# First attention: slot weights and values in tiles of 32 columns, scores and slot scores in tiles of 64

## The chip, the cores and the metric

The kernel runs on one core of a Trainium2 chip. The metric is the device time of one execution in microseconds; the median of some executions stands for a kernel. Within the core, TensorE (PE in the profile) multiplies matrices. Its weight loads (PEld) are instructions of their own and overlap the matmuls. VectorE (DVE), ScalarE (ACT) and GpSimd (POOL) work beside it; they wait for each other by semaphores.

## The reference, cut to what matters

The program is two transformer layers on `x` of 64 sequences, 32 tokens each, 256 channels. The change lies in the first attention, with 16 heads of 128 channels and 64 slots per head. Tokens see only their own sequence, and there only themselves and earlier tokens:

```python
A = jnp.einsum('bhtd,bhjd->bhtj', q, k) * scale      # scores
A = jnp.where(mask, A, 0.0)
ok = enz * jnp.einsum('bhtj,bhjm->bhtm', A, es)      # slot scores
qv = jax.nn.softmax(ok, axis=-1)
W2 = jnp.einsum('bhtm,bhjm->bhtj', qv * enz, es)     # slot weights
W2 = jnp.where(mask, W2, 0.0)
o = jnp.einsum('bhtj,bhjd->bhtd', W2, v)             # values
```

`mask` is lower triangular over the 32 tokens (T = 32) of a sequence. `A` and `W2` are therefore 32 x 32 matrices, one for each sequence and head.

## The kernel before

`attention0` works in 64 steps. A step `i` takes 128 token rows (one of G = 16 groups, four whole sequences, BPG = 4) and four of the heads (HQ = 4). The steps run over the 16 groups within each of the four quads of heads. Every engine has its own list of instructions, written out by hand and executed in order; what crosses engines is a semaphore wait.

In a step TensorE does, in this order (function, line): the transposes of the softmax (`turn_p`, L372), half of the output projection (`heads_out`, L420), the transposes of the gated output (`turn_og`, L372), **the slot weights** (`slot_weights`, L437), the other half of the output projection (L420), the transposes of `es` (`turn_es`, L372), **the scores** of the next step (`scores`, L391), **the values** (`values`, L449), **the slot scores** of the next step (`slot_scores`, L403), then one matmul for the slots (L362), the projections of v and gate (`project`, L330, twelve matmuls), and those of q and k (`quarter`, L319, twelve) with the running sums (L367, L368) in their middle.

The four functions in bold multiply many small matrices, and each places them in a part of the 128 x 128 array with `tile_position` (first row, first column of the array). All four use tiles of 64 x 64, which hold two sequences at once. The product of two sequences' tokens is 64 x 64, of which only the two diagonal blocks of 32 x 32 are wanted; the masks `mA` and `m01_own` (128 x 64 each) put zeros on the rest. `scores` and `slot_weights` take their 64 contracted rows from either half of the partitions (`e`) and write tokens to either half of the columns (`b`), four tiles in all; `slot_scores` and `values` contract over the 64 tokens of a pair of sequences, so only the two tiles on the diagonal are used.

A matmul of type f32 stands in the trace as two matmul and two weight-load records; one of type fp32r as one of each (the trace prints both as f32 on some lines). So 8 slot-weight matmuls are 16 records of L437.

VectorE multiplies the scores in PSUM by `mA` into `am` (`mask_scores`, L714), and the slot weights by `m01_own` into `wm` (`mask_weights`, L719). The scores and the slot weights share a pair of PSUM banks (`pair`, AW_TA in the trace), so `scores` waits for `mask_weights` (`w2_mask`). ScalarE copies v out of PSUM (`v_out`, L507, v_s) before TensorE may start `quarter` on the same bank.

Of the kernel before, what the change touches and what calls it, by code (L numbers as in the profile page):

```python
# [10 lines left out]
ALU = mybir.AluOpType  # L11
# [3 lines left out]
P = 128  # L15
B, T, D = 64, 32, 256
BPG = P // T
# [4 lines left out]
H0, DK, M0 = 16, 128, 64  # L22
HQ = 4
# [15 lines left out]
def attention0(nc, k, xres, x, cond, wcond, w_slices, wo, ws1, ws2b, ucol, gnorm, rope_cos, rope_sin, maskA, mask01, mask01_own):  # L39

    with ExitStack() as ctx:
        sb, psum, sem = k.tools(ctx)
# [4 lines left out]
        TW2 = 2 * T  # L47
# [19 lines left out]
        sinb = sb("sinb", [P, T])  # L67
        mA = sb("mA", [P, TW2])
        m01 = sb("m01", [P, P])
        m01_own = sb("m01_own", [P, TW2])  # L70
        idx_i = sb("idx_i", [B, 1], I32)
        u_col = sb("u_col", [RW, 1])
        turned = sb("turned", [P, 2, 2, 2, 2, TOK])
# [11 lines left out]
        enz = sb("enz", [P, SW])  # L85
        esT_s = sb("esT_s", [P, SW])
        am = sb("am", [P, HQ, TW2])
        wm = sb("wm", [P, HQ, TW2])
        ok = sb("ok", [P, SW])
        ex = sb("ex", [P, SW])  # L90
        exz = sb("exz", [P, SW])
# [3 lines left out]
        pT_s = sb("pT_s", [P, SW])  # L95
# [9 lines left out]
        pair = psum("AW_TA", [P, 2, QW])  # L105
# [12 lines left out]
        def heads(ap, n=HQ):  # L118
            return ap.rearrange("p (h d) -> p h d", h=n)

        both = pair[:, :, 0:2 * TW2].rearrange("p e (a t) -> p a e t", a=2)

        def by_pairs(ap):
            return ap[:, :, :].rearrange("p (a e) t -> p a e t", a=2)

        def for_heads(mask):
            return mask[:, :].unsqueeze(1).unsqueeze(1).to_broadcast([P, 2, 2, TW2])

        def turn_of(j):

# [36 lines left out]
        a_mm, a_mask = sem("a_mm"), sem("a_mask")  # L167
        ok_mm, ok_z, ok_min, ok_exp = [sem(n) for n in ("ok_mm", "ok_z", "ok_min", "ok_exp")]
        p_sum, p_eps, p_z = sem("p_sum"), sem("p_eps"), sem("p_z")
        w2_mm, w2_mask = sem("w2_mm"), sem("w2_mask")  # L170
# [119 lines left out]
        def _(pe):  # L290
# [3 lines left out]
            for g in range(G):  # L294
                if g == G // 2:
                    pe.wait_ge(x_more, 16)
                for c in range(KD):
                    m = pe.matmul(banks[g // 2][:, (g % 2 * KD + c) * P:(g % 2 * KD + c + 1) * P],
                                  xres[:, g, c * P:(c + 1) * P], bd[:, g, :], start=True, stop=True)
# [129 lines left out]
            def slot_weights(i):  # L429
                pe.wait_ge(pT_ev, i + 1)  # L430
                pe.wait_ge(esT_ev, i + 1)
                for a in range(2):
                    for b in range(P // TW2):
                        own = slice(a * P + b * TW2, a * P + (b + 1) * TW2)
                        for e in range(2):
                            rows = slice(e * M0, (e + 1) * M0)
                            m = pe.matmul(pair[b * TW2:(b + 1) * TW2, e, a * TW2:(a + 1) * TW2], esT_s[rows, own], pT_s[rows, own],  # L437
                                          start=True, stop=True, tile_position=(e * M0, b * TW2))
                m.then_inc(w2_mm, 1)

            def values(i):
                pe.wait_ge(w2_mask, i + 1)
                pe.wait_ge(v_ev, i + 1)
                pe.wait_ge(o_gate, i)
                pe.wait_ge(o_sq, i)
                for h in range(HQ):
                    for b in range(P // TW2):
                        toks = slice(b * TW2, (b + 1) * TW2)
                        m = pe.matmul(OO[toks, h * P:(h + 1) * P], wm[toks, h, :], v_s[toks, i % 2, h * P:(h + 1) * P],  # L449
                                      start=True, stop=True, tile_position=(b * TW2, b * TW2))  # L450
                m.then_inc(o_mm, 1)

            A = slice(0, None)
# [17 lines left out]
            for i in range(-1, STEPS):  # L471
                now, one, two = i >= 0, i + 1 < STEPS, i + 2 < STEPS
                if now:
                    turn_p(i)
                if i >= 2:
                    heads_out(i - 2, (0, 2))
                if i >= 1:
                    turn_og(i - 1)
                if now:
                    slot_weights(i)  # L480
                if i >= 2:
                    heads_out(i - 2, (2, HQ))
                if one:
                    turn_es(i + 1)
                    scores(i + 1)
                if now:
                    values(i)
                if one:
                    slot_scores(i + 1)
                if two:  # L490
                    slots(i + 2)
                if one:
                    proj_v(i + 1, A)
                    proj_g(i + 1, A)
                x1(i + 1 + FIRST)
                if two:
                    running(i + 2)
                x2(i + 1 + FIRST)
# [114 lines left out]
        def _(dve):  # L613
# [97 lines left out]
            def mask_scores(i):  # L711
                dve.wait_ge(a_mm, i + 1)
                dve.wait_ge(ok_mm, i)
                dve.tensor_tensor(by_pairs(am), both, for_heads(mA), ALU.mult).then_inc(a_mask, 1)  # L714

            def mask_weights(i):
                dve.wait_ge(w2_mm, i + 1)
                dve.wait_ge(o_mm, i)
                dve.tensor_tensor(by_pairs(wm), both, for_heads(m01_own), ALU.mult).then_inc(w2_mask, 1)  # L719

            for j in range(FIRST):
                x1_by_cos(j)
# [8 lines left out]
            for i in range(-1, STEPS):  # L731
                j, now, one, two = i + 1 + FIRST, i >= 0, i + 1 < STEPS, i + 2 < STEPS
                if now:
                    mask_weights(i)
                if now and one:
                    z(i + 1, 1)
                if i >= 2:
                    y_out(i - 2)
                if one:
                    mask_scores(i + 1)  # L740
                    slot_max(i + 1)
                if two:
                    clip(i + 2)
                if now:
                    norm_sum(i)
                    gated(i)
                if one:
                    slot_sum(i + 1)
                    silu(i + 1)
                if j < TURNS:  # L750
                    x1_by_cos(j)
                    x1_by_sin(j)
                if two:
                    z(i + 2, 0)
                if j < TURNS:
                    x2_by_both(j)
# [1224 lines left out]
def build(nc, a, out):  # L1981
    with ExitStack() as whole:
# [28 lines left out]
        with nc.Block() as block:  # L2011
            @block.sync
            def _(sp):
# [3 lines left out]
                sp.wait_ge(first, 48)  # L2017

        attention0(nc, k, xres, *[a[n] for n in ATT0])
        renew()  # L2020
        raw = sb("raw", [P, 3, KD * 1024])
# [61 lines left out]
def constants():  # L2083

    import numpy as np

    def rotary(width):
        inv = 1.0 / np.float32(10000.0) ** (np.arange(0, width, 2, dtype=np.float32) / width)
        angle = np.arange(T, dtype=np.float32)[:, None] * inv[None].astype(np.float32)
        c, s = np.cos(angle), np.sin(angle)  # L2090
        return np.tile(np.concatenate([c, c], 1), (BPG, 1)), np.tile(np.concatenate([-s, s], 1), (BPG, 1))

    j, t = np.arange(P)[:, None], np.arange(P)[None]
    seen = ((j // T == t // T) & (j <= t)).astype(np.float32)
    own = np.tile(seen[0:2 * T, 0:2 * T], (P // (2 * T), 1))
    inv0 = 1.0 / np.float32(10000.0) ** (np.arange(0, DK, 2, dtype=np.float32) / DK)
    turn0 = np.tile((np.arange(T, dtype=np.float32)[:, None] * inv0[None].astype(np.float32)).T, (2, 1))
    cos1, sin1 = rotary(4)
    later = np.where(np.arange(T)[None] > np.arange(T)[:, None], np.float32(-1e30), np.float32(0))
    return {  # L2100
        "identity": np.eye(P, dtype=np.float32), "ucol": (np.arange(RW) % (2 * RQ) == RS).astype(np.float32).reshape(RW, 1),
        "slot": np.where(np.arange(3 * 16) // 16 == 1, -1, np.arange(3 * 16) % 16).astype(np.float32).reshape(3 * 16, 1),
        "pcol": (np.arange(P) // 16).astype(np.float32).reshape(P, 1), "prow": np.arange(P, dtype=np.float32).reshape(P, 1),
        "rope_cos": np.cos(turn0), "rope_sin": np.sin(turn0),
        "mask_scale": own * np.float32(DK ** -0.5), "mask01": seen, "mask01_own": own,
        "cneg": np.tile(later, (BPG, 1)), "rcos1": cos1, "rsin1": sin1,
    }

# [16 lines left out]
```

## Time and profile before

| | us |
|---|---|
| median of 3 runs | 1463.17 |
| lowest, highest | 1461.98, 1464.67 |
| the profiled execution: its time | 1463.88 |
| its span in the profile | 1462.1 |
| PE busy | 1332.1 (91%) |
| PEld busy | 1065.6 (73%) |
| DVE busy | 938.1 (64%) |
| ACT busy | 517.3 (35%) |
| POOL busy | 556.4 (38%) |

The profile's times start at the beginning of the span; 1.8 us of the execution lie around it. The steps of the first attention fill the stretch from about 63 to 783 us. What follows (the first MLP, the second attention, the second MLP) is not touched by the change, and serves below only as a place where other sizes of tile can be seen. In a timeline row the first number is the start, the second the time from the first start to the last end of a merged group; matmul records overlap, so the pace is read from one group's start to the next group's start.

### The profile page before, as it was taken

The page shows a single profiled execution, that of the slowest core. Times are in us where ns is not written, and L with a number is a line of the kernel's source. Part 1 is how long each engine was busy: PE and PEld are TensorE (multiplying, and loading weights), DVE is VectorE, ACT ScalarE, POOL GpSimd, SP SyncE. Part 2 cuts the span into 40 slices and gives each one's busy share as a digit, 9 for nine tenths or more (in the row PEclk, how much of TensorE's full clock was granted, in tenths as well). Part 3 has the DMA queues.
Part 4 walks back from the last instruction along what each step waited for, and adds up shares of the span by engine and source line. Part 5 has one row for each costly group of instructions (what it writes and reads, how often), then busy time and mean ns, then how long its engine had stood idle before and what let it go on. Part 6 is the DMA issues. An engine that isn't in the chain of part 4 may idle for free. (4 is left out here: it accounts for less than half of the span.)

```text
span 1462.1 us, 36841 instructions
## 1 busy us (share of the span) xinstructions
PE 1332.1 (91%) x14806; PEld 1065.6 (73%) x14806; DVE 938.1 (64%) x1825; ACT 517.3 (35%) x1188; POOL 556.4 (38%) x608
## 2 busy tenths in 40 slices
PE   2899999999999999999986789999998788997996
PEld 2688888888888888888864577777776566775664
DVE  2787887888788878787864464252424245666786
ACT  2244444444444444444442213231312122222442
POOL 0665555565656565555531312122221111122111
PEclk9999999999999999999998899999999799997998
DMA  6000000000000000000002500000000630000610
GB/s 192 5 12 13 13 13 13 30 13 12 13 16 27 13 13 17 1 2 2 1 2 95 163 1 1 0 1 0 0 0 0 206 90 0 0 0 15 198 58 22
DMA packets 33376, 46.47 MB, mean 32 GB/s; under 512 B 6974, under 2 KB 22552, under 8 KB 32728
## 3 DMA queue, kind: packets, MB, share of 16 engines
q1 hardware_dynamic: 31048, 42.23, 9.5%
q10 hardware_dynamic: 2112, 2.10, 0.5%
q8 instruction: 93, 1.52, 0.4%
q14 instruction: 43, 0.35, 0.1%
q0 software_dynamic: 80, 0.26, 0.1%
HBM read 42.22 MB, written 2.36 MB: 30 GB/s over the span
## 5 line engine op out<-in xcount | busy, mean ns | idle before, releaser
L420 PE MATMUL OE<-w_o,ogT_s 128*128 128x256 f32 x512 | 139.5, 396 | 0.7 <-ACT ogT_s L507 0.7
L876 POOL TENSOR_TENSOR hT_lo<-h,hT_hi 128x512 fp32r<-128x512 f32 x44 | 56.8, 1291 | 192.9 <-ACT hT_hi L1049 192.9
L234 POOL TENSOR_TENSOR turned<-t1c,t2s 128x512 f32<-128x512 f32 x62 | 78.7, 1269 | 122.2 <-DVE t2s L637 122.2
L662 DVE RECIPROCAL enz<-SC 128x128 f32<-128x128 f32 x128 | 121.2, 948 | 2.9 <-PE SC L368 2.5
L1112 DVE SCALAR_TENSOR_TENSOR t<-th,m 128x512 f32<-128x512 f32 (+1 forms) x56 | 38.4, 685 | 121.3 <-ACT th L1054 93.5
L275 POOL TENSOR_TENSOR exz<-ex,enz 128x256 f32<-128x256 f32 x64 | 47.4, 741 | 160.9 <-ACT ex L573 160.9
L319 PE MATMUL PJ<-hs_hi,w_hi 128*128 128x512 f32 x248 | 102.4, 413 | 0.0
L330 PE MATMUL PJ<-w_hi,hs_hi 128*128 128x512 f32 x256 | 100.5, 392 | 0.0
L330 PE MATMUL PJ<-w_hi,hs_lo 128*128 128x512 f32 x256 | 100.1, 391 | 0.0
L330 PE MATMUL PJ<-w_lo,hs_hi 128*128 128x512 f32 x256 | 99.9, 390 | 0.0
L420 PEld LDWEIGHTS OE<-w_o,ogT_s 128*128 128x128 f32 x512 | 88.2, 192 | 12.4 <-ACT ogT_s L507 1.0
L319 PE MATMUL PJ<-hs_hi,w_lo 128*128 128x512 f32 x248 | 97.1, 392 | 0.0
L319 PE MATMUL PJ<-hs_lo,w_hi 128*128 128x512 f32 x248 | 96.9, 391 | 0.0
L573 ACT ACTIVATE ex<-ok,mn 128x64 f32<-128x64 f32 x256 | 68.3, 337 | 52.6 <-DVE mn L701 52.6
L507 ACT ACTIVATE pT_s<-AW_TA 128x256 f32<-128x256 f32 x64 | 24.6, 384 | 167.0 <-PE AW_TA L372 167.0
L1049 ACT ACTIVATE hT_hi<-h 128x512 fp32r<-128x512 f32 (+1 forms) x56 | 35.4, 632 | 124.4 <-DVE h L1118 124.4
L235 POOL TENSOR_TENSOR turned<-t2c,t1s 128x512 f32<-128x512 f32 x62 | 78.6, 1268 | 0.0
L242 POOL TENSOR_TENSOR og<-og,rstd 128x512 f32<-128x512 f32 x64 | 66.6, 1041 | 5.0
L449 PE MATMUL OO<-v_s,wm 64*64 64x128 f32 x1024 | 67.7, 269 | 0.0
L1308 POOL TENSOR_TENSOR r<-qk,raw 128x128 f32<-128x128 f32 x16 | 7.4, 463 | 156.5 <-DVE qk L1537 156.5
L239 POOL TENSOR_TENSOR rstd<-mse,mhalf 128x4 f32<-128x4 f32 x64 | 65.1, 1017 | 4.9 <-DVE mse L691 4.9
L666 DVE SCALAR_TENSOR_TENSOR gs<-gs,PJ 128x512 f32<-128x512 f32 x64 | 44.0, 687 | 34.6 <-ACT gs L528 34.6
(383 smaller groups left out, 3575.1 us busy)
## 6 DMA issues: line engine op xcount, KB each, us to landing
we_ring<-in_we SPq DMA_DIRECT2D x64, 256.0 KB, 3.1
w_raw<-in_w_slices SPq DMA_DIRECT2D x48, 128.0 KB, 2.2
turned<-in_w_slices ACTq DMA_DIRECT2D x4, 512.0 KB, 7.4
xres<-in_x SPq DMA_DIRECT2D x2, 1024.0 KB, 14.6
out_rows<-xres SPq DMA_DIRECT2D x16, 128.0 KB, 1.7
w1r<-in_w1i SPq DMA_DIRECT2D x1, 1408.0 KB, 6.5
w_s<-in_w SPq DMA_DIRECT2D x2, 682.0 KB
w_o<-in_wo SPq DMA_DIRECT2D x1, 1024.0 KB, 5.3
```

Source lines behind the costliest of these rows:

```text
L234: pool.tensor_tensor(to[:, 0, :], x1c[:, :], x2s[:, :], ALU.subtract)
L235: pool.tensor_tensor(to[:, 1, :], x2c[:, :], x1s[:, :], ALU.add).then_inc(qk_add, 1)
L239: pool.tensor_tensor(rstd[:, :], mse[:, :], mhalf[:, :], ALU.pow).then_inc(o_rstd, 1)
L242: pool.tensor_tensor(heads(og[:, :]), heads(og[:, :]), rstd[:, :].unsqueeze(2).to_broadcast([P, HQ, DK]), ALU.mult).then_inc(o_norm, 1)
L275: pool.tensor_tensor(exz[:, :], ex[:, :], enz[:, :], ALU.mult).then_inc(p_z, 1)
L319: m = pe.matmul(banks_of(j)[half][:, :], w[:, slot, a:a + P], h[:, c, toks], start=(n == 0), stop=(n == len(terms) - 1))
L330: m = pe.matmul(bank[:, :], h[:, c, toks], w[:, slot, a:a + QW], start=(n == 0), stop=(n == len(terms) - 1))
L420: m = pe.matmul(OE[:, SW:SW + D], ogT_s[:, i % 2, h * P:(h + 1) * P], w_o[:, i // G % 2, h, :], start=(h == 0), stop=(h == HQ - 1))
L449: m = pe.matmul(OO[toks, h * P:(h + 1) * P], wm[toks, h, :], v_s[toks, i % 2, h * P:(h + 1) * P], start=True, stop=True, tile_position=(b ...
L573: act.activation(ex[:, cols], ok[:, cols], ACT.Exp, scale=-1.0, bias=mn[:, h:h + 1]).then_inc(ok_exp, 1)
L662: dve.reciprocal(enz[:, cols], SC[:, SW:2 * SW][:, cols]).then_inc(z_rec, 1)
L876: eng.tensor_tensor(hT[1][s, m % 2, :], h[s, m % 2, :], hT[0][s, m % 2, :].bitcast(F32), ALU.subtract).then_inc(second, 1)
```

## The change

`slot_weights` and `values` go to tiles of 32 columns, one sequence each. The slot weights become 16 matmuls of 64 rows x 32 columns with 32 columns streamed (before 8 of 64 x 64 with 64), in eight tiles. The values become 16 matmuls of 32 x 32 with 128 columns streamed (before 8 of 64 x 64 with 128), in the four tiles on the diagonal. `wm` and the mask `m01_own` shrink from 64 to 32 columns, so `mask_weights` works on 128 x 128 instead of 128 x 256 elements; the view `both` takes its width as an argument. `scores`, `slot_scores` and `mA` stay as they are. The file is longer by one line, so numbers of lines from 122 on are one higher afterwards.

```diff
-        m01_own = sb("m01_own", [P, TW2])
+        m01_own = sb("m01_own", [P, T])
...
-        wm = sb("wm", [P, HQ, TW2])
+        wm = sb("wm", [P, HQ, T])
...
-        both = pair[:, :, 0:2 * TW2].rearrange("p e (a t) -> p a e t", a=2)
+        def both(width):
+            return pair[:, :, 0:2 * width].rearrange("p e (a t) -> p a e t", a=2)
...
-            return mask[:, :].unsqueeze(1).unsqueeze(1).to_broadcast([P, 2, 2, TW2])
+            return mask[:, :].unsqueeze(1).unsqueeze(1).to_broadcast([P, 2, 2, mask.shape[1]])
...
-                    for b in range(P // TW2):
-                        own = slice(a * P + b * TW2, a * P + (b + 1) * TW2)
+                    for b in range(BPG):
+                        own = slice(a * P + b * T, a * P + (b + 1) * T)
                         for e in range(2):
                             rows = slice(e * M0, (e + 1) * M0)
-                            m = pe.matmul(pair[b * TW2:(b + 1) * TW2, e, a * TW2:(a + 1) * TW2], esT_s[rows, own], pT_s[rows, own],
-                                          start=True, stop=True, tile_position=(e * M0, b * TW2))
+                            m = pe.matmul(pair[b * T:(b + 1) * T, e, a * T:(a + 1) * T], esT_s[rows, own], pT_s[rows, own],
+                                          start=True, stop=True, tile_position=(e * M0, b * T))
...
-                    for b in range(P // TW2):
-                        toks = slice(b * TW2, (b + 1) * TW2)
+                    for b in range(BPG):
+                        toks = slice(b * T, (b + 1) * T)
                         m = pe.matmul(OO[toks, h * P:(h + 1) * P], wm[toks, h, :], v_s[toks, i % 2, h * P:(h + 1) * P],
-                                      start=True, stop=True, tile_position=(b * TW2, b * TW2))
+                                      start=True, stop=True, tile_position=(b * T, b * T))
...
-                dve.tensor_tensor(by_pairs(am), both, for_heads(mA), ALU.mult).then_inc(a_mask, 1)
+                dve.tensor_tensor(by_pairs(am), both(TW2), for_heads(mA), ALU.mult).then_inc(a_mask, 1)
...
-                dve.tensor_tensor(by_pairs(wm), both, for_heads(m01_own), ALU.mult).then_inc(w2_mask, 1)
+                dve.tensor_tensor(by_pairs(wm), both(T), for_heads(m01_own), ALU.mult).then_inc(w2_mask, 1)
...
-        "mask_scale": own * np.float32(DK ** -0.5), "mask01": seen, "mask01_own": own,
+        "mask_scale": own * np.float32(DK ** -0.5), "mask01": seen, "mask01_own": own[:, 0:T] + own[:, T:2 * T],
```

On TensorE, from the transposes of the softmax to the matmul for the slots, in a step in the middle of the first attention. Each row gives the line, the output and its operands, the size of the output and how many matmuls stand in a row. Before:

```order
L372 MATMUL AW_TA<-ident,exz 128x128 x2
L420 MATMUL OE<-w_o,ogT_s 128x256 x2
L372 MATMUL TB<-ident,og 128x128 x4
L437 MATMUL AW_TA<-pT_s,esT_s 64x64 x8
L420 MATMUL OE<-w_o,ogT_s 128x256 x2
L372 MATMUL TB<-ident,es 128x128 x2
L391 MATMUL AW_TA<-turned 64x64 x16
L449 MATMUL OO<-v_s,wm 64x128 x8
L403 MATMUL OE<-es,am 64x64 x8
L362 MATMUL SC<-w_s,uT 128x256
```

On TensorE, the same place after the change:

```order
L373 MATMUL AW_TA<-ident,exz 128x128 x2
L421 MATMUL OE<-w_o,ogT_s 128x256 x2
L373 MATMUL TB<-ident,og 128x128 x4
L438 MATMUL AW_TA<-pT_s,esT_s 32x32 x16
L421 MATMUL OE<-w_o,ogT_s 128x256 x2
L373 MATMUL TB<-ident,es 128x128 x2
L392 MATMUL AW_TA<-turned 64x64 x16
L450 MATMUL OO<-v_s,wm 32x128 x16
L404 MATMUL OE<-es,am 64x64 x8
L363 MATMUL SC<-w_s,uT 128x256
```

Nothing moves; two groups have twice as many matmuls. The slot weights still stand between groups that use the whole array, but the values, in tiles of 32, now stand between two groups in tiles of 64.

## Rows read from the trace of the kernel before

**Rows 1.** Busy time of each engine in two stretches, with the granted clock (PEclk)
```profile
core 0: us, PE busy (x) PEld busy (x) DVE busy (x) ACT busy (x) POOL busy (x), PEclk, DMA share, GB/s
400.00:411.27 11.27, 11.27 (x134) 9.31 (x127) 9.03 (x18) 4.99 (x14) 7.77 (x9) 1.00 0.05 13
83.00:782.00 699.00, 689.94 (x7587) 568.02 (x7587) 549.33 (x1100) 304.60 (x789) 397.07 (x414) 1.00 0.04 12
```
**Rows 2.** Waits of TensorE's weight loads, 83 to 782 us: total us, times, longest
```profile
PEld PJ L319 <- ACT v_s L507: 13.9, 57, 0.3
PEld AW_TA L391 <- issue: 10.8, 62, 0.5
PEld AW_TA L437 <- issue: 10.4, 62, 0.2
```
**Rows 3.** Timeline of TensorE's matmuls in one step: start us, length us
```profile
407.42 0.38 PE L372 MATMUL AW_TA<-ident,exz 128*128 128x128 f32 x2
407.63 1.03 PE L420 MATMUL OE<-w_o,ogT_s 128*128 128x256 f32 x4
408.50 0.60 PE L372 MATMUL TB<-ident,og 128*128 128x128 f32 x4
409.03 0.46 PE L437 MATMUL AW_TA<-pT_s,esT_s 64*64 64x64 f32 x16
409.42 1.13 PE L420 MATMUL OE<-w_o,ogT_s 128*128 128x256 f32 x4
410.39 0.38 PE L372 MATMUL TB<-ident,es 128*128 128x128 f32 x2
410.70 0.69 PE L391 MATMUL AW_TA<-turned 64*64 64x64 f32 x32
...
412.09 0.62 PE L403 MATMUL OE<-es,am 64*64 64x64 f32 x15
```
**Rows 4.** The same, one step earlier, from the slot scores on
```profile
400.81 0.64 PE L403 MATMUL OE<-es,am 64*64 64x64 f32 x16
401.39 0.39 PE L362 MATMUL SC<-w_s,uT 96*128 96x256 f32 x1
401.61 0.39 PE L330 MATMUL PJ<-w_hi,hs_hi 128*128 128x512 f32 x1
```
**Rows 5.** Timeline of the weight loads of that step
```profile
409.02 0.33 PEld L437 LDWEIGHTS AW_TA<-pT_s,esT_s 64*64 64x64 f32 x16 [0.17 <-issue]
...
410.70 0.56 PEld L391 LDWEIGHTS AW_TA<-turned 64*64 64x64 f32 x32 [0.17 <-issue]
411.16 0.87 PEld L449 LDWEIGHTS OO<-v_s,wm 64*64 64x64 f32 x16
411.98 0.61 PEld L403 LDWEIGHTS OE<-es,am 64*64 64x64 f32 x16
```
**Rows 6.** Timeline of VectorE in that step, the two masks
```profile
409.56 0.42 DVE L719 TENSOR_TENSOR wm<-AW_TA,m_own 128x256 f32<-128x256 f32 x1 [0.25 <-PE AW_TA L437]
...
411.46 0.42 DVE L714 TENSOR_TENSOR am<-AW_TA,mA 128x256 f32<-128x256 f32 x1 [0.34 <-PE AW_TA L391]
```
**Rows 7.** Timeline of TensorE in the first step, the scores
```profile
73.37 0.69 PE L391 MATMUL AW_TA<-turned 64*64 64x64 f32 x32 [0.53 <-DVE wm L719]
73.86 1.08 PE L449 MATMUL OO<-v_s,wm 64*64 64x128 f32 x16
74.73 0.67 PE L403 MATMUL OE<-es,am 64*64 64x64 f32 x16
```
**Rows 8.** Timeline of TensorE in the second MLP: tiles of 64 rows, then 32 columns
```profile
1405.94 0.38 PE L1762 MATMUL Y<-be_s,hot_t 48*128 48x256 f32 x1
1406.26 1.07 PE L1766 MATMUL Y<-we_ring,xT 128*32 128x256 f32 x16
1407.26 0.44 PE L1752 MATMUL XY<-ident,xres 128*128 128x128 f32 x2
```
**Rows 9.** Timeline of TensorE in the second attention, tiles of 32 columns
```profile
1251.99 1.29 PE L1392 MATMUL S<-kT,qT 16*32 16x32 f32 x128
1253.64 0.59 PE L1360 MATMUL A<-xT,raw 128*128 128x128 f32 x3 [0.36 <-issue]
```
**Rows 10.** Timeline of TensorE in the first MLP, 42 rows after 128 rows
```profile
1057.76 0.40 PE L910 MATMUL m<-uum_hi,bu_lo 128*128 128x512 f32 x1
1057.99 0.39 PE L910 MATMUL m<-uum_lo,bu_hi 128*128 128x512 f32 x1
1058.31 0.39 PE L951 MATMUL m<-tern,hT_hi 42*128 42x256 f32 x1
```

## Prediction

> **What bounds the kernel now.** I read the stretches by engine first. In a step of the first attention TensorE is busy for all of its 11.27 us, at a granted clock of 1.00 (the 2.4 GHz level), while VectorE is busy for 9.03, GpSimd for 7.77 and ScalarE for 4.99 [rows 1]. Over 83 to 782 us, 62 steps, TensorE is busy 689.94 of 699.00 us. So the step is as long as TensorE's list of instructions, and the question is what the change does to that list. The waits of TensorE come next: one on another engine repeats in every step, the weight load of `quarter` that waits for ScalarE's copy of v (13.9 us in 57 times, 0.24 each); the other two that repeat are "issue" waits of 0.17 us, in front of the scores and of the slot weights [rows 2, 5]. Those two are what this change hangs on: they wait for no engine, and they stand exactly where the list goes from the whole array to tiles of 64.
>
> **The price of going from one size of tile to another.** Take the timeline of one step [rows 3]. Into tiles: two transposes take 407.63 - 407.42 = 0.21 us, so the four that start at 408.50 should hand over at 408.93; the slot weights start at 409.03, 0.10 late. Inside the tiles the second record of each matmul comes late once as well, since its weights weren't loaded ahead. The scores show that: 32 records take 411.21 - 410.70 = 0.51 us (the values start where their loads do, 411.16 to 411.21 [rows 5]), and at the pace of the slot scores, below, the 32 would take 0.46; that is 0.05. Out of tiles: the slot scores take 401.39 - 400.81 = 0.58 us [rows 4]. Their 16 records stream half of the columns that the values' 16 do, and the values take 74.73 - 73.86 = 0.87 [rows 7], some 0.054 a record; so the slot scores' own time is 0.44 to 0.46, and the step out 0.11 to 0.14. The first matmul behind it then holds the second up: the four records of the output projection take 1.13 us right behind the slot weights and 1.03 elsewhere [rows 3], 0.10 more. An excursion into tiles thus costs 0.15 in and 0.21 out.
>
> Is the same paid between two sizes of which neither is the whole array? No row of the first attention shows it. From scores to values to slot scores, all in 64 x 64, the loads show no idle time: the values' start at 411.16, before the scores end, and the slot scores' at 411.98 [rows 5]. The second MLP has the nearest place: a matmul of 48 rows is followed by tiles of 128 x 32. The first starts at 1405.94, the next at 1406.26, 0.32 later [rows 8]. The slots' matmul has the same 256 columns in one record, also stands first behind a step out of tiles, and hands over within the whole array after 401.61 - 401.39 = 0.22 [rows 4]. So 0.10 is paid there. That the number of rows alone is enough I read in the first MLP: 1058.31 - 1057.99 = 0.32 in front of 42 rows, and 0.23 in front of another 128 rows [rows 10]. I take it that 64 x 64 to 32 x 32 pays as well.
>
> The Trainium skill, TensorEngine Tiling (Array Packing), "Key Properties", says that a change of the tiling mode, not of the tile alone, drains TensorE. By that rule the values now cost two drains which they did not before; [rows 8] agrees with its 0.10 us.
>
> **The change part by part, for one step.** *Values.* Each tile still streams four heads of 128 columns, in two records each. With four tiles in place of two the records double, and four run side by side instead of two, so the 0.87 us stay. Less is excluded, since each tile streams as long as before; the upper end is that only two of the four tiles run at once, 1.74. That four tiles can share the array is seen in [rows 8]: 16 records of 256 columns in 1407.26 - 1406.26 = 1.00 us, where one after another, at the (408.50 - 407.63)/4 = 0.22 of such a record [rows 3], they would take 3.5. I take 0.
>
> *The two switches around the values.* In: 0.11, as late as elsewhere, and nothing for the second record, whose turn comes only 0.109 (0.87/8) later anyway, more than the load takes. Out, into the slot scores: 0.10, and 0.05 for the late second record, since these stream only 64 columns. Together 0.26. Bounds: 0 if 64 to 32 costs nothing, and 0.15 + 0.21 = 0.36 if each end costs what the costliest one does. I take 0.26 because [rows 8], another pair of partial sizes, shows a first part in full.
>
> *Slot weights.* They stand between whole-array groups before and after, so no switch is added. Before, 409.42 - 409.03 = 0.39 us, of which 0.11 to 0.15 is the step out [rows 3]. After there are 32 records of half the columns. The nearest row is the second attention's: 128 records of 32 columns within 1.29 us, of which about 0.19 is the last one's length, so 1.10/128 = 8.6 ns each [rows 9]; 32 of them take 0.28, less some 0.03 because the last tiles stream half as long on the way out. 0.28 + 0.11 - 0.03 = 0.36: a gain of 0.03. Bounds: a gain of 0.13 if half the columns halve the 0.25 that lies before the step out, and a loss of 0.23 if 32 records take what the 32 of the scores take, 0.51 + 0.11 against 0.39. I take -0.03, since [rows 9] has the same number of columns.
>
> *Mask of the weights on VectorE.* 0.42 us for 128 x 256 now; half of the elements, I put it at 0.25 to 0.30. It ends at 409.98 and the scores, which wait for it, start at 410.70 [rows 3, 6], so 0.7 us cover it and the gain is nothing. Only in the first two steps, where the output projection is missing, do the scores wait for it (0.53 in the first [rows 7], and once more): -0.3 us in all. If that cover fell away TensorE would wait, not gain. The mask of the scores (0.42, from 411.46) stays; the slot scores load at 411.98, right behind it [rows 5, 6]. It is released by the scores, so with the values later it gets more slack, not less. The load of `m01_own` is once, at the start, and half as large: nothing.
>
> *The wait for v.* It does not absorb the loss: ScalarE's copy of v stands behind the exponentials, these behind VectorE's work on the slot scores, all of it later by the same amount as TensorE. If it were fixed to something earlier, up to 0.09 a step would be hidden, 6 us.
>
> **The sum.** 63 steps have values between scores and slot scores: 63 x 0.26 = +16.4. 64 slot weights: 64 x -0.03 = -1.9. First steps: -0.3. Together +14.2 us, a step of 11.27 + 0.23 = 11.50. The profiled execution would go from 1463.88 to 1478.1 and its span from 1462.1 to 1476.3; the median is 0.7 lower, 1477.4. By the bounds, 0.15 to 0.36 for the switches (0 is rival 1) and -0.13 to +0.23 for the slot weights: 0.02 to 0.59 a step, 1464 to 1500.
>
> **The rivals.** (1) *No switch between 64 and 32.* The array may keep both sizes as one mode. For it: nothing in this kernel shows that very pair; against it [rows 8, 10]. Then only the slot weights' gain stays, -1.9 - 0.3: 1461. Chance 0.12. (2) *The same, and the slot weights run at full pace,* the case on the other side: with the 0.13 of their bound TensorE is that much shorter a step, and as it bounds the step [rows 1], 64 x 0.13 + 0.3 = 8.6 us come out, 1455. It decides for "faster" from 0.04 a step. It needs the switch to be free, as (1). Chance 0.05. (3) *Only two diagonal tiles run at once.* 0.87 more a step, 64 x 0.87 + 14 = +70: 1533. For it: [rows 8] has its four tiles in one block of rows, the values have four blocks of rows. Against it: the scores already use two blocks of rows and two of columns. Chance 0.05. (4) *Every small matmul has a floor.* The slot weights' 32 records would pay it one by one; against it the 8.6 ns in [rows 9]. At 27 ns a record, half of what one of the values' takes now, they would take 0.86 + 0.11 instead of 0.39: 0.58 a step, +37; with the switches' 16, 1516. The Trainium skill, TensorEngine Tiling, "Instruction Overhead", gives about 60 cycles for each matmul however few its columns; [rows 9] is against it for tiles that run side by side. Chance 0.03.
>
> **How the numbers follow.** The forecast, slower by about 14 us, gets 0.75, the rivals 0.25 as above. About 0.2% (3 us) is what a measurement can tell from no change. Slower: 0.75 + 0.05 + 0.03 = 0.83; same: 0.12; faster: 0.05. The range: 0.68 of the forecast's 0.75 lies within 1466 to 1488 (ends where both terms are at their bounds together are unlikely), and rival (1) at 1461 brings it to 0.80; above, (3), (4) and the forecast's tail are left out, below (2). So 1461 to 1488.
>
> **What would show it.** In the new profile: a step of 11.50 us; an "issue" wait or a gap of 0.1 in front of the values' weight loads and again in front of the slot scores'; the scores' start to the values' start 0.62 instead of 0.51; values to slot scores 0.97 instead of 0.87; slot weights to output projection 0.36; the mask of the weights below 0.30 us; the wait for v unchanged at 0.24. If the values' loads still start before the scores end, rival (1) holds. If values to slot scores takes 1.7, rival (3).

## The result, and the profile after

The change makes the kernel slower, as forecast, by a little less than forecast.

| | before | after |
|---|---|---|
| median us (6 runs each) | 1463.05 | 1475.5 |
| lowest, highest | 1461.2, 1464.67 | 1475.05, 1480.13 |
| ratio after / before, 95% interval | | 1.009, 1.0075 to 1.0105 |
| the profiled execution: its time, its span | 1463.88, 1462.1 | 1480.13, 1478.3 |

The forecast median was 1477.4, the measured one is 1475.5: +12.4 us instead of +14.2. The profiled execution of the kernel after is 4.6 us above its own median. Those microseconds don't lie in the changed stage. The values' matmul records (L449 before, L450 after, since the file is a line longer) end with a last start at 777.9 us before and 790.0 after, +12.1; what is left of the span behind them is 684.2 and 688.3 us, of code that the change doesn't touch. I therefore argue from the steps, whose length repeats from one to the next, and not from the span.

The last start stands in the view of one line's instructions, here that of the kernel before and then that of the kernel after:

```profile
L449 PE MATMUL OO<-v_s,wm x1024: 269/269/320, 73.9 to 777.9; 64*64 64x128 f32 x171
```

```profile
L450 PE MATMUL OO<-v_s,wm x2048: 264/268/292, 73.5 to 790.0; 32*32 32x128 f32 x187
```

The timeline of TensorE in one step after, to be read against [rows 3, 4] (start us, length us):

```profile
403.01 0.36 PE L438 MATMUL AW_TA<-pT_s,esT_s 64*32 64x32 f32 x32
403.30 1.13 PE L421 MATMUL OE<-w_o,ogT_s 128*128 128x256 f32 x4
404.26 0.38 PE L373 MATMUL TB<-ident,es 128*128 128x128 f32 x2
404.57 0.69 PE L392 MATMUL AW_TA<-turned 64*64 64x64 f32 x32
405.20 1.07 PE L450 MATMUL OO<-v_s,wm 32*32 32x128 f32 x32
406.20 0.68 PE L404 MATMUL OE<-es,am 64*64 64x64 f32 x16
406.82 0.39 PE L363 MATMUL SC<-w_s,uT 96*128 96x256 f32 x1
...
412.86 0.38 PE L373 MATMUL AW_TA<-ident,exz 128*128 128x128 f32 x2
```

| from start to start, us | before | after | difference (median over the steps, before rounding) |
|---|---|---|---|
| slot weights to output projection | 0.39 | 0.29 | -0.11 |
| scores to values | 0.51 | 0.63 | +0.11 |
| values to slot scores | 0.87 | 1.00 | +0.13 |
| slot scores to the slots' matmul | 0.58 | 0.62 | +0.04 |
| the step (softmax transposes at 401.40 to 412.86; before, [rows 1]) | 11.27 | 11.46 | +0.19 |

A step is 0.19 longer, and 63 steps of that are 12.0 us, which is what was measured. The four differences add up to 0.17 of it. The other 0.02 lie in the projections, where some matmuls follow each other a few ns later than before; why is open.

The weight loads of the same step show the mechanism. Against [rows 5], the slot scores' loads, which used to start before the values were done, now have an "issue" wait of 0.20 us; the values' loads start only at 405.20, with the values themselves:

```profile
404.57 0.56 PEld L392 LDWEIGHTS AW_TA<-turned 64*64 64x64 f32 x32 [0.17 <-issue]
405.20 0.81 PEld L450 LDWEIGHTS OO<-v_s,wm 32*32 32x32 f32 x32
406.20 0.54 PEld L404 LDWEIGHTS OE<-es,am 64*64 64x64 f32 x16 [0.20 <-issue]
```

And the waits of the weight loads over 83 to 790 us have one row more than [rows 2], the second one here. The wait for ScalarE's copy of v is nearly as it was:

```profile
PEld PJ L320 <- ACT v_s L508: 12.6, 57, 0.3
PEld OE L404 <- issue: 12.3, 62, 0.2
PEld AW_TA L392 <- issue: 10.6, 62, 0.4
PEld AW_TA L438 <- issue: 10.4, 62, 0.2
```

VectorE's mask of the weights takes 0.29 us instead of the 0.42 in [rows 6], and is over at 403.83, long before the scores at 404.57:

```profile
403.54 0.29 DVE L720 TENSOR_TENSOR wm<-AW_TA,m_own 128x128 f32<-128x128 f32 x1 [0.26 <-PE AW_TA L438]
```

### The profile page after: what moved, and what is told of

Read it like the earlier page. It is cut to its first block and busy times, and to the rows that moved or that the text cites. A ratio compares the mean times of both kernels' runs of the same rounds, so it can differ in the third digit from the quotient of the medians.

```text
span 1478.3 us, 40937 instructions
## 1 busy us (share of the span) xinstructions
PE 1347.6 (91%) x16854; PEld 1062.0 (72%) x16854; DVE 929.8 (63%) x1825; ACT 518.9 (35%) x1188; POOL 557.4 (38%) x608
## 5 line engine op out<-in xcount | busy, mean ns | idle before, releaser
L699 DVE SCALAR_TENSOR_TENSOR ok<-OE,enz 128x256 f32<-128x256 f32 x64 | 27.2, 425 | 75.4 <-PE OE L404 75.4
L450 PE MATMUL OO<-v_s,wm 32*32 32x128 f32 x2048 | 69.2, 271 | 0.0
```

## The experiments

Two theories were set against each other. S: what costs is the crossing from one size of tile to another, twice a step around the values, while the slot weights gain. R: what costs is that the narrow tiles need twice as many records. Every kernel in this section but the last is the kernel before or after with one edit. The step lengths below are medians over a kernel's steps of the distance between two starts of the scores. Where the text speaks of records one by one, it goes by the start of each single record in the trace, which the merged rows don't show.

**The values alone.** The kernel before with the values in 32 x 32 tiles; `wm` stays 64 wide, and each sequence reads its half of it.

```diff
-                    for b in range(P // TW2):
-                        toks = slice(b * TW2, (b + 1) * TW2)
-                        m = pe.matmul(OO[toks, h * P:(h + 1) * P], wm[toks, h, :], ...
+                    for b in range(BPG):
+                        toks = slice(b * T, (b + 1) * T)
+                        m = pe.matmul(OO[toks, h * P:(h + 1) * P], wm[toks, h, b % 2 * T:(b % 2 + 1) * T], ...
```

> Kernel before with the values alone in 32 x 32 tiles; slot weights and the mask stay 64 wide. Theory S (what costs is crossing from one size of tile to another, twice a step): the crossings are all there and the slot weights' gain is missing, so a step of 11.273 + 0.12 + 0.13 + 0.04 = 11.57 us, scores to values 0.63, values to slot scores 1.00, time about 1482. Theory R (what costs is that twice as many records run): the values' 32 records alone add less than the change's 64 do, a step between 11.27 and 11.45, and the 0.63 between the starts of scores and values isn't there.

Measured: median 1480.96 (4 runs), ratio to before 1.0113 (1.0087 to 1.014). A step is 11.56 us, and its timeline has the change's three losses and not its gain:

```profile
406.33 0.46 PE L437 MATMUL AW_TA<-pT_s,esT_s 64*64 64x64 f32 x16
406.72 1.13 PE L420 MATMUL OE<-w_o,ogT_s 128*128 128x256 f32 x4
408.00 0.69 PE L391 MATMUL AW_TA<-turned 64*64 64x64 f32 x32
408.62 1.08 PE L449 MATMUL OO<-v_s,wm 32*32 32x128 f32 x32
409.63 0.68 PE L403 MATMUL OE<-es,am 64*64 64x64 f32 x16
410.24 0.39 PE L362 MATMUL SC<-w_s,uT 96*128 96x256 f32 x1
```

The slot weights take 0.39 as before, scores to values 0.62, values to slot scores 1.01, slot scores 0.61. S had said 11.57. The whole loss comes with the values' tiles, and VectorE's shorter mask, which is missing here, played no part in it.

**The slot weights alone.** The kernel before with the slot weights in 64 x 32 tiles. Since the values still contract over two sequences, the mask has to write both halves of `wm`, which VectorE does in two instructions.

```diff
-                    for b in range(P // TW2):
-                        own = slice(a * P + b * TW2, a * P + (b + 1) * TW2)
...
-                            m = pe.matmul(pair[b * TW2:(b + 1) * TW2, e, a * TW2:(a + 1) * TW2], esT_s[rows, own], pT_s[rows, own],
-                                          start=True, stop=True, tile_position=(e * M0, b * TW2))
+                    for b in range(BPG):
+                        own = slice(a * P + b * T, a * P + (b + 1) * T)
...
+                            m = pe.matmul(pair[b * T:(b + 1) * T, e, a * T:(a + 1) * T], esT_s[rows, own], pT_s[rows, own],
+                                          start=True, stop=True, tile_position=(e * M0, b * T))
...
-                dve.tensor_tensor(by_pairs(wm), both, for_heads(m01_own), ALU.mult).then_inc(w2_mask, 1)
+                for a in range(2):
+                    m = dve.tensor_tensor(wm[:, 2 * a:2 * a + 2, :].rearrange("p e (c t) -> p e c t", c=2),
+                                          pair[:, :, a * T:(a + 1) * T].unsqueeze(2).to_broadcast([P, 2, 2, T]),
+                                          m01_own[:, :].rearrange("p (c t) -> p c t", c=2).unsqueeze(1).to_broadcast([P, 2, 2, T]),
+                                          ALU.mult)
+                m.then_inc(w2_mask, 1)
```

> Kernel before with the slot weights alone in tiles of 64 x 32; the values stay in 64 x 64, so the mask writes 64 columns of wm, as two VectorE instructions of 128x128. Theory S: no crossing is added, slot weights to output projection 0.29 instead of 0.39, a step of 11.17 us, 64 x 0.10 = 6.6 us out, time about 1456.5 (faster than both). The two mask instructions end before 410.3 on the scale of the kernel before and are hidden. Theory R: 32 records instead of 16 make the step longer than 11.273, time 1463 or more.

Measured: median 1457.36 (6 runs), ratio 0.9962 (0.995 to 0.9975): faster than both kernels. A step is 11.17 us.

```profile
406.39 0.35 PE L437 MATMUL AW_TA<-pT_s,esT_s 64*32 64x32 f32 x32
406.68 1.13 PE L420 MATMUL OE<-w_o,ogT_s 128*128 128x256 f32 x4
407.65 0.38 PE L372 MATMUL TB<-ident,es 128*128 128x128 f32 x2
407.96 0.69 PE L391 MATMUL AW_TA<-turned 64*64 64x64 f32 x32
408.47 1.05 PE L449 MATMUL OO<-v_s,wm 64*64 64x128 f32 x16
409.35 0.64 PE L403 MATMUL OE<-es,am 64*64 64x64 f32 x16
409.92 0.39 PE L362 MATMUL SC<-w_s,uT 96*128 96x256 f32 x1
```

The slot weights take 0.29; scores to values is back at 0.51, values to slot scores at 0.88, slot scores at 0.57. So the change was in the main the sum of a gain of 0.11 and a loss of 0.29 a step (together 0.18 of the 0.19), and they can be had apart. The two mask instructions together take 0.49 and end 0.54 us before the scores start:

```profile
406.93 0.49 DVE L720 TENSOR_TENSOR wm<-AW_TA,m_own 128x128 f32<-128x128 f32 x2 [0.26 <-PE AW_TA L437]
```

**Twice the values' records without a crossing.** The kernel before; each values' matmul is cut into two of 64 columns, the tiles stay 64 x 64.

```diff
-                        m = pe.matmul(OO[toks, h * P:(h + 1) * P], wm[toks, h, :], v_s[toks, i % 2, h * P:(h + 1) * P],
+                        for c in range(2):
+                            cols = slice(h * P + c * M0, h * P + (c + 1) * M0)
+                            m = pe.matmul(OO[toks, cols], wm[toks, h, :], v_s[toks, i % 2, cols],
```

> Kernel before with each of the values' matmuls cut into two of 64 columns, still in 64 x 64 tiles: as many records as in the change (32), no crossing. Theory S: scores to values stays 0.51; values to slot scores 0.87 plus the pace of records of 64 columns (0.029 each instead of 0.054 for 128: 32 x 0.029 = 0.93), so a step of 11.31 to 11.35. Theory R: the whole of the values' loss, 0.29, comes with the records: 11.56.

Measured: median 1468.68 (4 runs), ratio 1.0038 (1.0022 to 1.0054), a step of 11.37 us.

```profile
402.90 0.69 PE L391 MATMUL AW_TA<-turned 64*64 64x64 f32 x32
403.41 1.15 PE L451 MATMUL OO<-v_s,wm 64*64 64x64 f32 x32
404.35 0.68 PE L403 MATMUL OE<-es,am 64*64 64x64 f32 x16
404.96 0.39 PE L362 MATMUL SC<-w_s,uT 96*128 96x256 f32 x1
```

Scores to values stays at 0.51, and values to slot scores is 0.93 as the median, 0.06 more, as S said. The step is a little above S's range (11.31 to 11.35), because the slot scores take 0.61 instead of 0.58 here too, with no crossing in front of them. So the length of that group alone is no proof of a crossing; the starts of single records tell the two cases apart. In the change the second pair of the slot scores' records starts 0.11 us after the first, where later pairs come every 0.06: that is the late second record behind a crossing. Here none is late, but the two tiles run 54 ns out of step with each other, where it was 20 in the kernel before, and so the last record starts 0.03 later. R loses: doubling the records adds 0.09 to the step here, where the change's values lost 0.29.

**One crossing less.** The kernel after with the slot scores in 32 x 32 tiles as well, so that only the crossing from scores to values is left.

```diff
-                    for b in range(P // TW2):
-                        toks = slice(b * TW2, (b + 1) * TW2)
-                        m = pe.matmul(OE[toks, h * M0:(h + 1) * M0], am[toks, h, :],
-                                      es[toks, h * M0:(h + 1) * M0], start=True, stop=True, tile_position=(b * TW2, b * TW2))
+                    for b in range(BPG):
+                        toks = slice(b * T, (b + 1) * T)
+                        m = pe.matmul(OE[toks, h * M0:(h + 1) * M0], am[toks, h, b % 2 * T:(b % 2 + 1) * T],
+                                      es[toks, h * M0:(h + 1) * M0], start=True, stop=True, tile_position=(b * T, b * T))
```

> Kernel after with the slot scores in 32 x 32 tiles too (16 matmuls of 64 columns), so that values and slot scores have the same size and one of the two crossings is gone; the scores stay in 64 x 64. Theory S: values to slot scores falls from 1.00 to about 0.89, the slot scores' late second record goes as well (0.04), and a step is 11.467 - 0.11 - 0.04 = 11.32 us, time about 1466. Theory R: 16 records more, so a step of 11.467 or more, time 1475 or more.

Measured: median 1466.02 (10 runs), ratio to before 1.0022 (1.001 to 1.0035), a step of 11.33 us.

```profile
399.79 0.57 PE L392 MATMUL AW_TA<-turned 64*64 64x64 f32 x25
400.28 1.08 PE L450 MATMUL OO<-v_s,wm 32*32 32x128 f32 x32
401.18 0.62 PE L404 MATMUL OE<-es,am 32*32 32x64 f32 x32
401.74 0.39 PE L363 MATMUL SC<-w_s,uT 96*128 96x256 f32 x1
```

Values to slot scores is 0.90 instead of 1.00, slot scores 0.56 instead of 0.62, although 16 records were added. With the same size on both sides, the crossing's 0.11 is gone, and no second record of the slot scores is late any more. (The 25 records of the scores are those inside the window that was read.)

**Four crossings.** The kernel before; the values of the first and third head go in 32 x 32 tiles, those of the second and fourth in 64 x 64.

```diff
-                    for b in range(P // TW2):
-                        toks = slice(b * TW2, (b + 1) * TW2)
-                        m = pe.matmul(OO[toks, h * P:(h + 1) * P], wm[toks, h, :], v_s[toks, i % 2, h * P:(h + 1) * P],
-                                      start=True, stop=True, tile_position=(b * TW2, b * TW2))
+                    w = T if h % 2 == 0 else TW2
+                    for b in range(P // w):
+                        toks = slice(b * w, (b + 1) * w)
+                        own = slice(b * w % TW2, b * w % TW2 + w)
+                        m = pe.matmul(OO[toks, h * P:(h + 1) * P], wm[toks, h, own], v_s[toks, i % 2, h * P:(h + 1) * P],
+                                      start=True, stop=True, tile_position=(b * w, b * w))
```

> Kernel before, with the values of the first and third head of a step in 32 x 32 tiles and those of the second and fourth in 64 x 64: 24 records instead of 16, and four crossings between the sizes instead of none (the change has two, with 32 records). Theory S (each crossing has its price): 0.107 to 0.110 each for letting the array run empty and 0.024 for the late second record behind it, 4 x 0.13 = 0.53, a step of 11.80 us, time about 1496. Theory R (the doubled records cost): half of the records that values32 adds, so half of its 0.28, a step of 11.42, time about 1472.

Measured: median 1497.97 (2 runs), ratio 1.024 (1.022 to 1.0261), a step of 11.83 us.

```profile
402.59 0.69 PE L391 MATMUL AW_TA<-turned 64*64 64x64 f32 x32
403.22 1.50 PE L451 MATMUL OO<-v_s,wm 32*32 32x128 f32 x24
404.55 0.63 PE L403 MATMUL OE<-es,am 64*64 64x64 f32 x16
```

With fewer records than the change (24) and twice its crossings, the step loses 0.56 us against 0.29 in the first experiment. Scores to values is 0.63, and the values take 1.33: 0.46 more than the 0.87 of before, three crossings inside them at 0.15 each. A crossing thus costs 0.11 to 0.15 us, and the costs add up. The 0.11 is the gap itself: the first record behind each of the three starts 0.20 us after the last one ahead of it, where a round of the values otherwise follows after 0.09. The rest is the late second record.

**Why the slot weights gain.** The kernel before; each slot-weight matmul is cut into two of 32 columns, in the same four tiles of 64 x 64.

```diff
-                            m = pe.matmul(pair[b * TW2:(b + 1) * TW2, e, a * TW2:(a + 1) * TW2], esT_s[rows, own], pT_s[rows, own],
-                                          start=True, stop=True, tile_position=(e * M0, b * TW2))
+                                m = pe.matmul(pair[b * TW2:(b + 1) * TW2, e, a * TW2 + c * T:a * TW2 + (c + 1) * T], esT_s[rows, own],
+                                              pT_s[rows, own.start + c * T:own.start + (c + 1) * T],
+                                              start=True, stop=True, tile_position=(e * M0, b * TW2))
```

(`c` runs over 0 and 1 between `b` and `e`.)

> Kernel before with each slot-weight matmul cut into two of 32 columns, still in the four 64 x 64 tiles: 32 records of 32 columns as in the change, but not eight tiles. If the gain of 0.106 us in the slot weights comes from eight tiles side by side: slot weights to output projection stays at 0.39 or grows, a step of 11.27 to 11.40. If it comes from shorter records as such: 0.29, a step of 11.17.

Measured: median 1477.03 (2 runs), ratio 1.0097 (1.0077 to 1.0118), a step of 11.50 us.

```profile
403.57 0.69 PE L438 MATMUL AW_TA<-pT_s,esT_s 64*64 64x32 f32 x32
404.19 1.13 PE L420 MATMUL OE<-w_o,ogT_s 128*128 128x256 f32 x4
```

The 32 records now take 0.62, way out included, where the kernel before took 0.39 and 64 x 32 tiles take 0.29. Cutting the records shorter gained nothing in this order of matmuls. The step is above what I had expected (11.27 to 11.40).

The edit changed more than the length of the records, though. With `c` between `b` and `e`, four matmuls in a row go to the two tiles of one `b` before the other two get any; the kernel before goes through all four tiles in turn. The single records fit that. Before, four start 7 ns apart and the next four 58 ns after them. Here two start 7 ns apart and the next two some 30 ns after them. So two tiles seem to be at work at a time, each with a new record of 32 columns every 30 ns, half of the 58 ns of a record of 64 columns; a tile of the values has one of 128 columns every 109 ns. By these numbers a tile's pace follows the columns streamed, and the group's time how many tiles work side by side: two here, four before, eight in 64 x 32 tiles. That is worked out from the record starts and was not tested: short records that go through all four tiles in turn were not run. Whether the narrower weight load (32 columns instead of 64) has a part in the gain is open. All that the runs show is that in a 64 x 64 tile a record with its load of 64 columns fits into 30 ns.

**Everything in tiles of 32 columns.** The kernel after with the scores in 64 x 32 and the slot scores in 32 x 32 tiles, `am` and `mA` 32 wide.

```diff
-                        for b in range(P // TW2):
-                            own = slice(toks.start + b * TW2, toks.start + (b + 1) * TW2)
+                        for b in range(BPG):
+                            own = slice(toks.start + b * T, toks.start + (b + 1) * T)
...
-                                m = pe.matmul(pair[b * TW2:(b + 1) * TW2, e, a * TW2:(a + 1) * TW2], turned[rows, q % 2, 1, a, s, own],
+                                m = pe.matmul(pair[b * T:(b + 1) * T, e, a * T:(a + 1) * T], turned[rows, q % 2, 1, a, s, own],
```

> Kernel after with the scores (64 x 32 tiles, 64 records) and the slot scores (32 x 32) in narrow tiles too, both masks 32 wide. The crossing between values and slot scores is gone, as in slotscores32 (11.333). Left is one from 64 rows to 32 rows at equal 32 columns. If a change of rows alone also drains, scores to values stays 0.11 above the pace of the scores; if not, a step 0.11 shorter. The scores' 64 records of 32 columns in eight tiles at 5 to 8.6 ns take 0.32 to 0.55 against 0.51 now, so with the drain a step of 11.14 to 11.37 us and a time of 1454 to 1468, without it 11.03 to 11.26.

Measured: median 1480.08, ratio 1.0118 (1.0098 to 1.0138), 4 runs, outside the range. Most steps are 11.40 us, and a dozen are 0.4 to 1.4 longer than their neighbours. First a step as most are, then one of the others:

```profile
303.48 0.76 PE L392 MATMUL AW_TA<-turned 64*32 64x32 f32 x64
304.22 1.08 PE L450 MATMUL OO<-v_s,wm 32*32 32x128 f32 x32
305.09 0.65 PE L404 MATMUL OE<-es,am 32*32 32x64 f32 x32
305.67 0.39 PE L363 MATMUL SC<-w_s,uT 96*128 96x256 f32 x1
```

```profile
407.27 0.76 PE L392 MATMUL AW_TA<-turned 64*32 64x32 f32 x64
408.03 1.08 PE L450 MATMUL OO<-v_s,wm 32*32 32x128 f32 x32
408.90 0.65 PE L404 MATMUL OE<-es,am 32*32 32x64 f32 x32
410.19 0.39 PE L363 MATMUL SC<-w_s,uT 96*128 96x256 f32 x1 [0.64 <-issue]
```

The scores' 64 records take 0.74 (0.72 as the median), 0.1 more than the 32 do in the kernel after (0.63), so the narrow tiles lose here what they gain in the slot weights. The first 32 start 5 ns apart on average, the last 32 10 ns apart.

In the second step TensorE stands still for 0.64 us behind the slot scores and waits for nothing that the profile shows. The 64 + 32 records of scores and values follow one another within 1.61 us (0.74 + 0.87), 17 ns each, and the slot scores' 32 come right behind. Nine of the twelve stops lie within or right behind the slot scores, two in the values, one in the projections. The likely reading is that the engine's supply of instructions runs dry, and the profile speaks for it. DMA queue q8 brings instructions in packets of 16 KB. In every kernel here it has one packet more for each 64 matmuls of type f32 that the edit adds, so these are TensorE's. First the kernel before, then this one (packets, MB, share):

```profile
q8 instruction: 93, 1.52, 0.4%
```

```profile
q8 instruction: 133, 2.18, 0.6%
```

In the first attention they come every 7.1 us on average here and every 11.2 before, and all twelve stops end 2.2 to 2.8 us after one of them started. Most packets bring no stop, and no run changed the supply alone, so the cause is not shown.

Does going from 64 x 32 to 32 x 32, a change of rows alone, have a price? The length of the scores can't say, but the single records can. The first record of the values starts 0.156 us after the last one of the scores. That is 0.038 in the kernel before, without a crossing, and 0.148 in the kernel after, from 64 x 64 to 32 x 32. So it has one here, of about 0.1.

## Why the prediction was right, and where it was not

**What bounds the kernel.** Right. TensorE filled the step before and after, each difference on it came out in the step, and no other engine's time mattered. VectorE's mask fell by 0.13 us in the change and rose by 0.07 in the experiment with the slot weights alone, and neither was seen in the step. Only the first two steps wait for it: 0.53 + 0.31 us before, 0.51 + 0.19 after, a gain of 0.1 where the forecast had 0.3.

**The price of a crossing between two partial sizes.** Right in kind, and nearly in size. The step "I take it that 64 x 64 to 32 x 32 pays as well" rested on [rows 8, 10] alone. The change showed it, the kernel with one crossing less took 0.11 out again, and the one with four had twice the loss. The term was 0.26 for both crossings; the profile gives 0.11 + 0.13 + 0.04 = 0.28. The single records show its parts: 0.11 for each of the two gaps, as forecast (0.11 and 0.10), and 0.05 for the late second record of the slot scores, as forecast. One part was wrong: I had said that the late second record behind the first crossing would cost nothing, since the values' records are long, and it adds 0.02. And 0.01 comes off, because the two tiles of the slot scores now run 7 ns out of step instead of 20.

**The values themselves.** Right at 0: with the crossing taken off, 32 records in four diagonal tiles take 0.90 in the kernel whose slot scores are narrow too, against 0.87, and the difference is the late second record just named. Once under way, four records of 32 x 32 start every 109 ns, two of 64 x 64 before. Rival (3), only two tiles at once, would have shown 1.7.

**The slot weights.** The term that was mis-sized: -0.03 forecast, -0.11 measured, 4.9 us over the 64 steps. The step that failed was the choice of row: "8.6 ns each [rows 9]" is the average pace of 128 records, and 32 records in a row don't meet whatever holds 128 up; in the last kernel above, too, the scores' first 32 records come twice as fast as the next 32. Here 0.29 - 0.12 for the way out leaves 0.17 for 32 records, some 5 ns each. The bound of -0.13 held it. The other bound, the scores' 0.51 + 0.11, was far off: 32 records start faster in eight tiles than the scores' 32 in four.

**The sum.** -0.03 + 0.26 = 0.23 forecast for a step, against -0.11 + 0.28 + 0.02 (in the projections) = 0.19. That the time came out within 2 us is in part luck: a gain larger by 0.08 stood against a loss larger by 0.02 and another 0.02 that no term had. The forecast's own terms already held the better kernel: the slot weights stand between whole-array groups and pay no new crossing, so their gain, small as I took it, could be kept alone.

**The wait for v.** It absorbed next to nothing: 12.6 us in 57 times, before 13.9, so 0.22 a time instead of 0.24. The rivals (1), (2) and (4) fell: the first two with the 0.20 us "issue" wait in front of the slot scores, the fourth with 5 ns a record.

The Trainium skill, TensorEngine Tiling (Array Packing), "Key Properties", says that a change of the tiling mode drains TensorE. By the measured 0.11 to 0.15 us a crossing, between 64 x 64 and 32 x 32 as well, the runs agree.

## What to carry to other kernels

Count the crossings between sizes of tile in the order of the matmuls, not only the matmuls: each cost 0.11 to 0.15 us here, and a group that is faster alone can lose more than it gains when its neighbours keep another size. Narrow the tiles first where a group already stands between whole-array groups: for the slot weights that alone gave 0.38%, the best kernel of this study (1457.36). It is no rule for long groups: the scores' 64 narrow records took longer than their 32 wide ones. And when two edits come in one change, price and try them one at a time; a loss of 0.29 hid a gain of 0.11.

## What the runs showed of the hardware that was not expected

How fast small matmuls go seems to depend on how many tiles work side by side, and so on their order too. In a 64 x 64 tile a record of 64 columns comes every 58 ns and one of 32 columns every 30. Yet 32 records of 32 columns took 0.62 us with the way out where their order kept two tiles at work (by the starts of the records), and 0.29 in eight tiles of 64 x 32.

A change of the tile's rows alone, from 64 x 32 to 32 x 32, has a gap of 0.156 us in front of it, much like the 0.148 from 64 x 64 to 32 x 32.

Kernels with very many small matmuls have stops of their own. With 96 records within 1.61 us and 32 more behind them, a dozen of the 64 steps were 0.4 to 1.4 us longer, with no wait on another engine, and each stop ended 2.2 to 2.8 us after a packet of TensorE's instructions had started. The length of the run alone doesn't bring it: 128 records in 1.29 us pass without a stop in [rows 9].
